# Layer two's bias of a mixture-of-experts block leaves the matmul chain: ScalarE scales it by the gate, GpSimd adds it

## The reference, cut to what matters

```python
x = x + gnn(layernorm(x), adj, ...)          # quantized graph layer: two matmuls
# then, with x_flat = layernorm(x):
logits = x_flat @ Wr + br
topk_w, topk_idx = top_k(softmax(logits), 2)          # 2 of 16 experts for each row
topk_w = topk_w / sum(topk_w)
h = einsum('nc,ech->neh', x_flat, W1) + b1
h = gelu(layernorm(h) * g1 + be1)
expert_out = einsum('neh,eho->neo', h, W2) + b2
y = sum over the 2 chosen experts of expert_out * topk_w
x = x + y
```

## Time and profile before

| what | value |
|---|---|
| median of three runs | 531.89 us (531.49 to 533.54) |
| the profiled execution | 533.34 us, its span 531.6 us |
| PE busy | 481.1 us (90%) |
| DVE, ACT, POOL busy | 349.1, 289.8, 227.2 us (66, 55, 43%) |
| mean granted TensorE clock | 0.967 of full speed |
| bytes moved | 87.75 MB, 165 GB/s over the span |
| expert part | from about 230 us to the end |

### The profile page before, as it was taken

How to read it: one execution, slowest core, us unless ns; L and a number is a source line. 1 busy time by engine, 2 the same in 40 slices (tenths; PEclk the granted TensorE clock), 3 DMA queues, 4 the chain that set the end, 5 groups by cost and what they waited for, 6 DMA issues and landing times. The chain is left out here.

```text
span 531.6 us, 10326 instructions
## 1 busy us (share of the span) xinstructions
PE 481.1 (90%) x2328; PEld 391.1 (74%) x2329; DVE 349.1 (66%) x699; ACT 289.8 (55%) x484; POOL 227.2 (43%) x302
## 2 busy tenths in 40 slices
PE   1789999899999997678999999999999999999981
PEld 0568888788877776657788788888777888778851
DVE  5797765656557568858665786676877766776420
ACT  1656453454343343526667667668768766665540
POOL 5583520411351726334544444444444444344432
PEclk9989999999999999559999999999999999999996
DMA  8621232654787441156766776776887896644443
GB/s 285 243 81 40 80 99 78 239 208 166 251 275 259 152 170 49 37 160 203 236 160 153 201 199 151 218 167 149 239 279 206 249 279 161 141 79 80 80 62 40
DMA packets 33033, 87.75 MB, mean 165 GB/s; under 512 B 6032, under 2 KB 6176, under 8 KB 32880
## 3 DMA queue, kind: packets, MB, share of 16 engines
q1 hardware_dynamic: 18912, 56.53, 32.4%
q0 software_dynamic: 9488, 22.55, 21.0%
q10 hardware_dynamic: 4608, 8.39, 4.1%
HBM read 68.05 MB, written 19.40 MB: 165 GB/s over the span
## 5 line engine op out<-in xcount | busy, mean ns | idle before, releaser
L865 ACT ACTIVATE g_sb<-ps,be_sb,g_sb 128x128 f32<-128x128 f32 x160 | 60.1, 456 | 63.6 <-PE ps L1486 62.9
L625 POOL DMA_INDIRECT xg<-xn_rows,tok_i x41 | 44.6, 1087 | 116.4 <-ACT gate L844 100.0
L1329 PE MATMUL ps<-sup,adj_hi 128*128 128x512 f32 x192 | 78.3, 408 | 2.3 <-DVE adj_lo L962 2.3
L1223 DVE TENSOR_TENSOR w_lo<-w_raw,w_hi x58 | 67.8, 1221 | 17.0 <-issue 17.0
L1329 PE MATMUL ps<-sup,adj_lo 128*128 128x512 f32 x192 | 75.3, 392 | 0.0
L962 DVE SCALAR_TENSOR_TENSOR adj_lo<-adj_raw,small,adj_hi 128x1024 fp32r<-128x1024 f32 x32 | 40.7, 1273 | 39.6 <-ACT adj_hi L705 39.5
L650 POOL DMA_INDIRECT out<-y_sb,scat_i x37 | 58.9, 1592 | 16.6 <-issue 10.4
L837 ACT ACTIVATE w_hi<-w_raw x29 | 54.8, 1914 | 1.8 <-DMA w_raw<-in_w 1.0
L581 POOL TENSOR_SCALAR rstd<-mv 128x1 f32<-128x1 f32 x15 | 14.6, 974 | 91.1 <-DVE mv L1008 91.1
L1230 DVE TENSOR_SCALAR h_hat<-ps,h_mv,h_rs 128x512 f32<-128x512 f32 x40 | 32.3, 807 | 28.6 <-issue 17.5
L705 ACT ACTIVATE adj_hi<-adj_raw,small 128x1024 fp32r<-128x1024 f32 x32 | 36.8, 1149 | 22.3 <-PE ps L1329 13.5
(11 more groups left out here) (181 smaller groups left out, 970.4 us busy)
## 6 DMA issues: line engine op xcount, KB each, us to landing
w_raw<-in_w SPq DMA_DIRECT2D x64, 512.0 KB
adj_raw<-in_adj_steps SPq DMA_DIRECT2D x32, 512.0 KB, 3.5
out<-x_sb ACTq DMA_DIRECT2D x16, 256.0 KB, 2.9
xn_rows<-xn ACTq DMA_DIRECT2D x16, 256.0 KB, 2.8
x_sb<-in_x SPq DMA_DIRECT2D x3, 1024.0 KB, 13.5
gw_raw<-in_gnn_w SPq DMA_DIRECT2D x1, 1024.0 KB, 5.0
x_sb<-in_x SPq DMA_DIRECT2D x2, 512.0 KB, 7.6
xg<-xn_rows,tok_i POOLq DMA_INDIRECT x41, 5.5
```

Of the source, the lines that this page charges most:

```text
L625: return pool.indirect_dma_start(to[:, s % 2, :], None, xn_rows, bass.IndirectOffsetOnAxis(ap=tok_i[:, s:s + 1], axis=0)).then_inc(landed[ ...
L865: ins = act.activation(g_sb[:, par, c * P:(c + 1) * P], ht_ps(par)[:, c * P:(c + 1) * P], ACT.Gelu, scale=g1_sb[:, bass.ds(e_s * C + c, 1) ...
L1223: ins = dve.tensor_tensor(w_lo[:, n, at], w_raw[:, n, :, :].rearrange("p a n -> p (a n)")[:, at], w_hi[:, n, at].bitcast(F32), ALU.subtract)
L1329: ins = pe.matmul(acc_bank(t), part[:, n % 2, k * P:(k + 1) * P], sup[:, first_k + k, :], start=first_k + k == 0 and part is adj_hi, stop= ...
```

## The change

Layer two's bias leaves TensorE. It is no longer split into two rows; `b2[e]` is loaded from the input and repeated over all 128 partitions (`b2_rows`, a 256 KB transfer in place of 4 KB), ScalarE writes `gated_bias = b2_rows * gate` right behind y and only then signals `y_ok`, and GpSimd adds it to `y_sb` in front of each scatter and waits for that add before it issues the scatter. The bias of layer one stays as it was.

The second edit moves half of layer two's low part: of the two halves of `w_lo` for n=1 the first stays in slot s, the second goes to slot s+1, behind layer one's halves of that slot, and `split_lo[1]` is signalled there. The vector and scalar queues read the plan word of the trip before as well (one more `load_plan` a trip). One memset of 2048 columns on GpSimd and one bias store pair fall away in the first part.

```diff
             def load_bias(n, e, ring):
-                sp.dma_start(bias_row[n][0:2, ring].bitcast(F32), bias_dram[n, e]).then_inc(raw_in[n], 16)
+                if n:
+                    row = e if not isinstance(e, int) else slice(e, e + 1)
+                    sp.dma_start(b2_rows[:, ring], b2[row, :].broadcast_to([P, D])).then_inc(raw_in[n], 16)
+                else:
+                    sp.dma_start(bias_row[0:2, ring].bitcast(F32), bias_dram[e]).then_inc(raw_in[n], 16)
...
-                if t in (AHEAD - 1, AHEAD + 1):
-                    pool.memset(bias_row[(t - AHEAD + 1) // 2][:, :].bitcast(F32), 0.0).then_inc(bias_zero, 1)
+                if t == AHEAD + 1:
+                    pool.memset(bias_row[:, :].bitcast(F32), 0.0).then_inc(bias_zero, 1)
...
-            def add_rows(at, par):
+            def add_rows(s, at, par):
+                pool.tensor_tensor(y_sb[:, par, :], y_sb[:, par, :], gated_bias[:, par, :], ALU.add).then_inc(y_biased, 1)
+                pool.wait_ge(y_biased, s + 1)
                 pool.sem_inc(pool_turn, 1)
                 pool.indirect_dma_start(
...
-            def gated(n, par, landed):
+            def gated(n, par, landed, e):
 
                 act.wait_ge(mm2, n + 1)
                 act.wait_ge(scattered[par], landed)
-                act.activation(y_sb[:, par, :], y_ps(par), ACT.Copy, scale=gate[:, bass.ds(n + 1, 1)]).then_inc(y_ok, 1)
+                act.activation(y_sb[:, par, :], y_ps(par), ACT.Copy, scale=gate[:, bass.ds(n + 1, 1)])
+                act.activation(gated_bias[:, par, :], b2_rows[:, bass.ds((e & 3) * D, D)], ACT.Copy,
+                               scale=gate[:, bass.ds(n + 1, 1)]).then_inc(y_ok, 1)
...
+            def low_piece(n, e, h):
+
+                at = bass.ds(((e + 1) & 1) * (C * D) + h * (C * D // 2), C * D // 2)
+                return dve.tensor_tensor(w_lo[:, n, at], w_raw[:, n, :, :].rearrange("p a n -> p (a n)")[:, at],
+                                         w_hi[:, n, at].bitcast(F32), ALU.subtract)
+
+            def begin_split(e, start):
+
+                with dve.If(start == 1):
+                    dve.wait_ge(split_hi[1], e + 2)
+                    low_piece(1, e, 0)
+
+            def end_split(e, start):
+
+                with dve.If(start == 1):
+                    low_piece(1, e, 1).then_inc(split_lo[1], 1)
...
                 split_next(0, expert_in(word, par + 2), starts_in(word, par + 2))
-                split_next(1, expert_in(word, par), starts_in(word, par))
+                if earlier is not None:
+                    end_split(expert_in(earlier, 1 - par), starts_in(earlier, 1 - par))
+                begin_split(expert_in(word, par), starts_in(word, par))
...
-                    word = load_plan(dve, j)
+                    earlier, word = load_plan(dve, j - 1), load_plan(dve, j)
...
-                pe.matmul(dst, two_rows[:, :], bias_row[n][:, bass.ds((e & 3) * D, D)], start=True, stop=False)
+                if not n:
+                    pe.matmul(dst, two_rows[:, :], bias_row[:, bass.ds((e & 3) * D, D)], start=True, stop=False)
                 for c in range(C):
-                    pe.matmul(dst, act_hi[:, par, c * P:(c + 1) * P], w_hi[:, n, at[c]], start=False, stop=False)
+                    pe.matmul(dst, act_hi[:, par, c * P:(c + 1) * P], w_hi[:, n, at[c]], start=n == 1 and c == 0, stop=False)
```

More of the change, by code:

```diff
@@ L257, in gnn_moe_program @@
         end_gnn = where[0]
-        bias_row = [place(f"bias_row{n}", [P, 4 * D], F32R) for n in (1, 2)]
+        bias_row = place("bias_row", [P, 4 * D], F32R)
+        b2_rows = place("b2_rows", [P, 4 * D], F32)
         where[0] = end_fixed
@@ L281, in gnn_moe_program @@
         assert where[0] <= hits_at
+        where[0] = hits_at
+        gated_bias = place("gated_bias", [P, 2, D], F32)
         where[0] = hits_at
@@ L370, in gnn_moe_program @@
         idx_ok = sem("idx_ok")
+        y_biased = sem("y_biased")
         rows_ok = sem("rows_ok")
@@ L486, in store_biases @@
                 sp.wait_ge(bias_ok, 1)
-                for n in range(2):
-                    for h, half in enumerate((bias_hi, bias_lo)):
-                        sp.dma_start(bias_dram[n, :, h, :], half[32 * n:32 * n + E, :].bitcast(F32)).then_inc(bias_out, 16)
+                for h, half in enumerate((bias_hi, bias_lo)):
+                    sp.dma_start(bias_dram[:, h, :], half[0:E, :].bitcast(F32)).then_inc(bias_out, 16)
             def first_weights(i):
@@ L682, in give_last @@
                 pool.wait_ge(y_ok, rest * 2 + (4 + back))
-                add_rows(idx_s[:, back:back + 1], par)
+                add_rows(rest * 2 + (1 + back), idx_s[:, back:back + 1], par)
             pool.tensor_copy(idx_s[:, :], scat_i[:, bass.ds(rest * 2 + 1, 3)]).then_inc(idx_ok, 1)
@@ L858, in _, with slot @@
             split_next(0, expert_in(word, 1), starts_in(word, 1))
-            def slot(s, par, word, landed, last=False):
+            def slot(s, par, word, landed, e_before, last=False):
                 e_s, e_a = expert_in(word, par), expert_in(word, par + 2)
@@ L880, in _ @@
             act.sem_inc(y_ok, 2)
-            slot(0, 0, word, None)
-            slot(1, 1, word, 16)
+            slot(0, 0, word, None, None)
+            slot(1, 1, word, 16, expert_in(word, 0))
             with act.Fori(1, SLOTS // 2 - 1) as j:
                 with act.If(j < rest + 1):
-                    word = load_plan(act, j)
+                    before, word = expert_in(load_plan(act, j - 1), 1), load_plan(act, j)
                     for par in range(2):
-                        slot(j * 2 + par, par, word, j * 16 + 16 * par)
-            word = load_plan(act, rest + 1)
+                        slot(j * 2 + par, par, word, j * 16 + 16 * par, expert_in(word, 0) if par else before)
+            before, word = expert_in(load_plan(act, rest), 1), load_plan(act, rest + 1)
             for par in range(2):
-                slot(rest * 2 + (2 + par), par, word, rest * 16 + (16 + 16 * par), last=True)
-            gated(rest * 2 + 3, 1, rest * 16 + 32)
+                slot(rest * 2 + (2 + par), par, word, rest * 16 + (16 + 16 * par), expert_in(word, 0) if par else before,
+                     last=True)
+            gated(rest * 2 + 3, 1, rest * 16 + 32, expert_in(word, 1))
         @block.vector
@@ L1262, in _ @@
                     own.enter(j - 1, 2 * 2)
-                    word = load_plan(dve, j)
+                    earlier, word = load_plan(dve, j - 1), load_plan(dve, j)
                     for par in range(2):
-                        slot(j * 2 + par, par, word)
+                        slot(j * 2 + par, par, word, word if par else earlier)
                     own.leave(0)
-            word = load_plan(dve, rest + 1)
+            earlier, word = load_plan(dve, rest), load_plan(dve, rest + 1)
             slot_h_hat(rest * 2 + 3, 1)
             slot_g_lo(rest * 2 + 2, 0)
+            end_split(expert_in(earlier, 1), starts_in(earlier, 1))
             split_next(1, expert_in(word, 0), starts_in(word, 0))
```

21 lines of the change are left out of this document (10 added, 11 removed).

## The result

The changed kernel takes **572.88 us** (median of 4 runs, 570.27 to 573.51); the kernel before, run beside it, 531.69 (531.21 to 533.54). The ratio is 1.0743, 95% interval 1.0717 to 1.0769: +41.2 us where +7 was forecast. The direction was right and the time is far outside the range of 527 to 544.5. The profiled span is 571.7 us against 531.6.

The account below looks back on a forecast made before the run. TensorE was taken to set the pace. Terms -8.8 (matmul), -1.3, -0.5, +1.2 (three-half slots), +12.0 (slots 17 to 26) and +4.5 (tail) gave +7.1 on 531.9: 539.0 us, 8-in-10 range 527 to 544.5.

Parts of the forecast that it names:

- The slot without a wait: TensorE's matmul chain: removing the bias matmul saves 0.23 us a slot, making it 6.63 us; -8.8 us over 38 slots.
- The tail: Last three scatters: each is later by its add on GpSimd, +4.5 us, the scatters 7.4 and 3.2 us apart.
- The add: GpSimd's 128x512 add of the gated bias: 1.3 us, bounds 0.6 and 2.4; another estimate gave 1.1 to 1.2.
- The wait of TensorE in slot 21: Second half of `w_lo` late behind `w_hi`, whose load is six us late: 8.8 us stall in place of 3.5.
- the clock: TensorE's clock at its lower level of 0.50 behind the long stall in slot 21: +1.8 us.
- The second wait on `w_lo`: TensorE waits for the second half made in slot 25, after an expert of one slot: 1.7 us.
- The head: Early part: slots 1 to 3 gain -1.3 us; one GpSimd memset falling away in the graph stage gives -0.5.
- Hidden, in a slot without `w_lo`: GpSimd's chain: counted from slot start H, `h_rs` runs at H+3.8 to 4.4, `h_hat` ends H+5.3, needed H+6.63; no cost.
- rival 3: GpSimd's add costs 2.4 us: +3.3 in the tail, +1 in first-of-expert slots behind a landing wait; 543 us, chance 0.10.
- the bytes: The 256 KB more in front of the late w1 load before slot 21: 1.0 us.
- Rival 4: GpSimd's add is locked out under VectorE's halves in some nine slots, delaying scatter and `h_hat`: +10, 549 us, chance 0.07.
- The sum: All terms give +7.1 us, 539.0 us; the two edits meet in slots 17 to 26, which cost +12.0 us.

Follow-up runs that it names:

- The pieces alone: The kernel before with only the second edit, layer two's low half made in two successive slots, the bias as it was: 541.2 us, +8.0.
- 4 KB rows: The changed kernel with each load of layer two's bias row sent to 2 partitions in place of 128: 565.9 us; leaving out GpSimd's add too, 539.8 us.
- without the add: The changed kernel with GpSimd's add and the wait for it left out: 546.0 us, +13.9 against the kernel before.
- the root first: The changed kernel, complete, with GpSimd's add and the root for three slots on placed ahead of the landing waits and the scatter: 557.2 us.
- leaving the power out: The changed kernel with layer norm's power on GpSimd removed, VectorE writing the variance where the root stood: 559.1 us.
- the bias edit with the root first: The kernel before with the bias change only, add and root ahead of GpSimd's landing waits and scatter: 543.1 us, +11.6.
- The order of the halves: The changed kernel with the second piece of the low half ahead of layer one's halves in VectorE's order: 565.4 us.
- beside a memset: The kernel before with the bias change only, a memset of 1440 columns of an unused tile in place of GpSimd's add: 544.8 us.
- the bias edit alone: The changed kernel with layer two's low half made in one slot again: 547.8 us, +14.6; leaving out GpSimd's add too, 528.1 us.
- its place in the queue: The bias change with VectorE making y times gate plus gated bias, no GpSimd add: 529.1 us behind `gt_lo`, 555.2 us behind the statistics.

## Why the prediction was wrong

**Right, by its own steps.** The slot without a wait is 6.63 us. The tail: +4.4, where +4.5 less the two matmuls saved in it makes 4.0; its scatters are 6.7 and 3.6 us apart. The add: 1.33 us for 1.3, above the other estimate of 1.1 to 1.2. The wait of TensorE in slot 21: 8.98 us for 8.8 (its listed terms add up to 8.5), behind a `w_hi` that stood 7.5 us for its load where six were forecast; the clock behind it 0.54 in 409 to 413 us, and the whole slot 17.74 us long, 2.1 more than 6.63 + 8.98. The second wait on `w_lo` is 1.1 for 1.7. The pieces alone, +8.0 with a wait of 6.4 in that slot, bear the mechanism out. In part the 8.98 is luck: with 4 KB rows it is 6.1, and 7.0 for 9.1 without the add, so the large bias rows have 2 to 3 us of it, and the forecast gave them 1.0. The head, 2.1 us ahead at slot 3 where -1.3, -0.5 and two slots of -0.23 make 2.3, says little: slot 3 starts anywhere from 257.4 to 261.5 us in the kernels of the experiments.

**The step that failed** is GpSimd's: `h_rs` at H+3.8 to 4.4, `h_hat` at H+5.3, "Hidden, in a slot without `w_lo`". The times hold in a slot like 13 (`h_rs` at H+4.2). But they start from a scatter that waits for nothing, as the one in the earlier trace rows. In 8 slots GpSimd waits for an earlier scatter's landing first (20.2 us in all; before it was 6.2 in 3), and 1.33 + 0.84 us of add and issue come behind that wait, with `h_rs` behind both. The text knew of the landing wait and gave it +1 us in all, in rival 3. It was not asked how long a landing is when the scatter itself is later and the queues are fuller. Shown by the root first (-16.1) and by leaving the power out (-14.2), some of either being the hold on VectorE. That there is a second way, through `y`'s buffer, is seen in the bias edit with the root first, which keeps +11.6; how much of that is the add's is open.

**A term left out: the bytes.** 256 KB more per expert were priced once, as 1.0 us ahead of one load. Cutting them gives 6.2 to 7.4 us.

**A second term too small: the clock.** The forecast had +1.8 us for it, behind one stall. It is low behind the long waits for `h_hat` as well, 6 to 10 us in all by the estimate above.

**A rival too low.** Rival 4 took the hold between GpSimd and VectorE as the add being held. The runs show it the other way too: VectorE's `gt_lo` is held by the add, 1.28 us for 0.69 in the mean, and TensorE waits for it. The Trainium skill, "SBUF — State Buffer", section "Who interferes with whom", says that two such instructions exclude each other, that a GpSimd instruction which only writes SBUF does not take part, and that the order of issue decides who is blocked. The trace agrees on the first (17 `gt_lo` beside an add) and the second (12 beside a memset, none longer than 0.69). On the order it does not: 13 of the 17 are shown to begin 0.14 to 0.51 us ahead of the add, and they are the ones held, though starts on GpSimd are rough. The price here, 3 to 5 us, is near the width of the intervals.

**The order of the halves** was priced rightly as a wait. That 7.9 us of the total hung on the order and not on the split was not seen.

**The sum.** The prediction treated the two edits as neighbours in slots 17 to 26. Their differences add to 22.6 and together they cost 41.2: without the add 10.9 of the 18.6 us between them are there already. The DMA share in 440 to 460 us is 0.58 before, 0.78 with the pieces alone and 0.89 here. The 4 KB rows show 6.2 to 7.4 us that hang on the bytes, with shorter waits for loads in both kernels, and for landings in the one without the add (27.9 to 20.2 us). That fuller queues and longer landings make the rest of the meeting too is argued.

## What to carry to other kernels

When an operation is put into the queue of an engine that also waits for transfers, cost it in the slot in which that wait is longest, not in a quiet one, and list everything that stands behind it there; here an add of 1.3 us, in the bias edit alone, cost 19.6. Ask of each small operation that a faster engine needs (the root) whether it can stand ahead of the waits. And put a bias where it is one operand more of an operation that is done anyway, then try its place in the queue, which was worth 26 us here.

## What the runs showed of the hardware that was not expected

A scatter that waits for GpSimd's own add is issued 0.84 us behind its end in most slots, and 0.84 behind the memset as well; where the root stands between, the scatter is issued 0.31 to 0.48 behind the root's end. The hold works from GpSimd on VectorE: `gt_lo`, begun 0.51 us ahead of the add, ended only 0.57 behind it, and the 16 others that overlapped an add in that kernel ended 0.55 to 0.56 behind theirs; a memset of the same length held none. VectorE's `y` from PSUM with two further operands takes 745 ns, 0.06 us more than ScalarE's with one (688).
